# V through the other PSUM bank pair and VectorE, the front of each tile one iteration earlier, four tiles in the first three iterations

## The chip, the core and the metric

The kernel runs on one core of one Trainium2 chip. The metric is the device time of one execution in microseconds (us), the median of several runs. Engines are called as in the profile: PE is TensorE (PEld its weight load), DVE is VectorE, ACT is ScalarE, POOL is GpSimd, and SP is the queue that issues nearly all DMAs. PSUM has eight banks of 128 x 512 floats.

## What is computed

Two layers with residuals on x of 4 x 2048 x 256 floats, cut to what matters:

```
x0 = layernorm(x)                       # no weights
xn = layernorm(x0) * ln1_w + ln1_b
q, k, v = xn @ wq + bq, xn @ wk + bk, xn @ wv + bv     # 16 heads of 16
fq, fk = elu(q) + 1, elu(k) + 1
kv = einsum('bhnd,bhne->bnde', fk, v)   # for each token n over its heads
qkv = einsum('bhnd,bnde->bhne', fq, kv)
attn = qkv / (fq . (fk summed over the heads) + 1e-6)
y = x0 + attn @ wo + bo
h = gelu((layernorm(y) * ln2_w + ln2_b) @ fc_w + fc_b)
z1 = x + y + h @ proj_w + proj_b
z = layernorm(z1)
gates = softmax of the top 2 of 8 experts, from the mean of z over the 2048 tokens of a sequence
out = z1 + sum over experts of gate * gelu(z @ expert_w + expert_b)
```

(In the kernel the sum in the denominator comes out of the same matmuls as `qkv`, through a column of ones beside V.)

## The kernel before

The 8192 tokens are cut into 16 tiles of 512. A tile passes through stages, and each iteration of a hand-written schedule runs stages of several tiles. `LAG` says how many iterations behind its own number a tile reaches a stage: with LAG 0 iteration i works on tile i, with LAG 2 on tile i - 2. `iterations()` lists the stages of each iteration in order, and `walk()` replays that list for every engine, so each engine executes the stages that it has a part in, in exactly this order. An engine waits at semaphores; `INC` tells how much each stage adds to each of them, and `at(name)` is the value that a semaphore has when all stages ahead in the list are done. Nothing reorders: whoever waits holds all that stands behind it on the same engine. The stages that the change and the prediction speak of:

- **L** loads x of a tile (SP) into a ring of 4. **DS** takes its statistics (DVE, with the power on POOL), **D1** normalizes it (DVE) to `xhat`, **X** transposes it (PE) and ACT copies it to `xhT`. X, DV, DQ and DK are called the front of a tile here.
- **DV** multiplies V (PE) into the banks `sa` (two of the four banks of `ps`). ACT copies them to `feat_v` (L480), POOL adds the bias `bv` (L430), and SP stores the result to DRAM in eight DMAs (L327). `feat_v` is one buffer: ACT waits for the stores of the tile before (`v_out`). **DQ** and **DK** multiply Q and K (PE, into `pw` and `sa`), ACT and DVE make elu + 1 of them (`fqk`), SP stores them in two DMAs each (L333).
- **K0**, **K1** load the halves of q and k back in another layout (SP, 8 DMAs each, L356), behind the landing of all q and k stores listed ahead of them (`q_out`, `k_out`). **VL** loads V back (SP, 8 DMAs, L345).
- **B0**, **B8** are the scores of half 0 (PE, all four banks `ps`, masked by DVE at L658). **B1** to **B4** (merged with the MLP's rounds C1 to C4 as M1 to M4) are: B1 the weighted sums of half 0, B2 the scores of half 1, B3 the weighted sums of half 1. ACT evicts the sums to `ot`, **NS0**, **NS1** store them, **NL0**, **NL1** load them back transposed (SP).
- **N0** divides half 0 on DVE (L687, L690), **N** half 1, and casts and splits the result for a float32r matmul (L697, L698). **A2** multiplies it by w_o (PE, L986) into `sb`, the other two banks of `ps`, and DVE adds it to the residual (L708). **R** normalizes on DVE, **H** transposes (PE), M1 to M4, **J7** are the MLP.
- **Z** normalizes, **E** transposes z (PE, into `sb`) and ACT evicts it to `zT` (L518). **G** is the pooled gate at the end of a batch (iterations 7, 11, 15, the head iterations). **F1**, **F3**, **F2** are the experts.
- **WV** makes the bias `bv`, **WS** multiplies ln2_b by the MLP's weights (PE, L850) and folds and splits the weights on DVE (L631 to L643). It is in iteration 1, between the first and the second tile.

A full iteration (7 to 15) is `MERGED` and then a tail:

```python
TAIL = ["DV", "DQ", "DK", "A2", "F1", "R", "B0", "F3", "F4", "SA", "H", "B8", "FX", "F2"]
HEAD_TAIL = ["XL", "E", "X", "J7", "JA", "YB", "G", "N", *TAIL]
FULL_TAIL = ["XL", "X", "J7", "JA", "YB", "E", "N", *TAIL]
```

In iterations 3 to 6 (`EARLY`) A2 stands ahead of DK.

## Time and profile before

| | |
|---|---|
| median of 3 runs | 1098.13 us (1096.04 to 1101.01) |
| the profiled execution | 1095.77 us, its span 1093.9 us |
| PE busy | 953.9 us, 87% |
| DVE busy | 701.5 us, 64% |
| ACT busy | 472.2 us, 43% |
| POOL busy | 238.4 us, 22% |

Times in the trace are us from the start of the span. The first MLP round (M1) starts at 115.30 in iteration 3; a full iteration takes 56 to 60 us, a head iteration 64 to 67. A row of a timeline is start, duration, engine, line, operation, output<-inputs, and how many instructions were merged; in brackets stands how long the engine was idle before it and what it waited for. SPq is SP's DMA queue: its duration is that of issuing, not that of the transfer. The granted clock of PE is at one of two levels, 1.2 or 2.4 GHz.

### The profile page before, as it was taken

How to read it: one execution, taken by the hardware profiler on the slowest of the kernel's cores; microseconds unless marked ns; L12 is line 12 of the kernel's file. 1: busy time of each engine (PE TensorE's matmuls, PEld its weight loads, DVE VectorE, ACT ScalarE, POOL GpSimd, SP SyncE). 2: the span in 40 equal slices, each digit the busy share in tenths (PEclk: the TensorE clock that was granted, in tenths of full speed). 3: DMA queues.
4: the chain of work that ended last, by engine and by line, in shares of the span. 5: the costliest groups of instructions: out<-in, count | busy, mean ns of one | idle time of the engine just before them, and what ended most of it. 6: DMA issues, size and time to landing. Idle time of an engine off the chain costs nothing.

```text
span 1093.9 us, 29184 instructions
## 1 busy us (share of the span) xinstructions
PE 953.9 (87%) x12212; PEld 737.0 (67%) x12212; DVE 701.5 (64%) x1560; ACT 472.2 (43%) x738; POOL 238.4 (22%) x144
## 2 busy tenths in 40 slices
PE   4764888989698989999999989999999899897866
PEld 3543776768586767768686857777777768685633
DVE  2724565766557567777868586777777775856523
ACT  2321444535253444545545434545454454342422
POOL 3220132311314131312222131223131220312000
PEclk9866887989698889999999999999999899898979
DMA  5667354555545465565656574565666555431013
GB/s 178 106 131 120 85 91 100 98 117 95 119 89 91 105 121 122 104 159 88 150 108 130 125 131 113 112 148 107 143 107 137 110 112 116 93 88 58 33 64 116
DMA packets 428696, 120.85 MB, mean 110 GB/s; under 512 B 389904, under 2 KB 414608, under 8 KB 428304
## 3 DMA queue, kind: packets, MB, share of 16 engines
q1 hardware_dynamic: 426256, 116.83, 50.9%
q10 hardware_dynamic: 2304, 2.11, 0.7%
q8 instruction: 98, 1.61, 0.6%
q14 instruction: 38, 0.31, 0.1%
HBM read 60.17 MB, written 58.72 MB: 109 GB/s over the span
## 4 chain that ended last, share of the span: by engine, by line
PE 65%; DVE 18%; issue 8%; DMA 3%; ACT 3%; POOL 2%; SPq 1%; ACTq 0%; DVEq 0%; POOLq 0%
PE pw L936 18%; PE pj L920 13%; PE ps L892 7%; PE pw L840 5%; PE ps L986 4%; PE pj L840 4%; PE ps L905 4%; DVE nd L690 4%; DVE nd L687 4%; PE ps L872 3%; PE ps L881 2%; DVE hT L698 2%; DVE x_sb L723 2%; DVE hT L697 2%; PE pj L1030 1%
## 5 line engine op out<-in xcount | busy, mean ns | idle before, releaser
L936 PE MATMUL pw<-hT,w_fc 128*128 128x512 f32 x768 | 213.7, 419 | 10.4 <-DVE hT L678 10.4
L920 PE MATMUL pj<-w_pj,hidden 128*128 128x256 f32 x1536 | 208.7, 285 | 2.7 <-DVE hidden L671 2.7
L920 PEld LDWEIGHTS pj<-w_pj,hidden 128*128 128x128 f32 x1536 | 197.5, 190 | 14.1 <-DVE hidden L671 3.7
L671 DVE TENSOR_TENSOR hidden<-xhT,hidden 128x512 fp32r<-128x512 f32 x128 | 88.5, 692 | 165.2 <-ACT hidden L506 165.1
L505 ACT ACTIVATE xhT<-pw,col 128x512 f32<-128x512 f32 x128 | 87.8, 686 | 228.4 <-PE pw L936 227.0
L936 PEld LDWEIGHTS pw<-hT,w_fc 128*128 128x128 f32 x768 | 144.3, 199 | 43.0 <-DVE hT L678 12.1
L658 DVE TENSOR_TENSOR am<-ps,mask 128x512 f32<-128x512 f32 x128 | 79.3, 681 | 63.7 <-PE ps L892 63.7
L892 PE MATMUL ps<-kq 16*64 16x64 f32 x4096 | 87.8, 314 | 20.9 <-issue 10.9
L892 PEld LDWEIGHTS ps<-kq 16*64 16x64 f32 x4096 | 77.3, 210 | 42.4 <-issue 40.4
L986 PE MATMUL ps<-w_o,hT 128*128 128x256 f32 x384 | 61.5, 326 | 31.6 <-DVE hT L698 31.1
L506 ACT ACTIVATE hidden<-pw,col 128x512 fp32r<-128x512 f32 x128 | 87.1, 680 | 0.0
L986 PEld LDWEIGHTS ps<-w_o,hT 128*128 128x128 f32 x384 | 57.3, 229 | 43.7 <-DVE hT L698 28.5
L436 POOL TENSOR_TENSOR x<-x,row 128x1024 f32<-128x1024 f32 x16 | 37.7, 2354 | 216.3 <-DVE x_sb L723 216.3
L513 ACT ACTIVATE ot<-ps,den_eps 128x512 f32<-128x512 f32 x64 | 69.4, 1192 | 33.7 <-PE ps L905 32.7
L872 PE MATMUL ps<-w_qkv,xhT 128*128 128x256 f32 x256 | 70.2, 436 | 3.2 <-ACT xhT L470 3.2
L840 PE MATMUL pw<-zT,w_e 128*128 128x512 f32 x128 | 60.6, 618 | 8.1 <-DMA b_e<-in_eb 8.1
L430 POOL TENSOR_TENSOR feat_v<-feat_v,bv 128x512 f32<-128x512 f32 x32 | 52.7, 1664 | 56.1 <-ACT feat_v L480 56.1
L872 PEld LDWEIGHTS ps<-w_qkv,xhT 128*128 128x128 f32 x256 | 56.0, 225 | 13.0 <-issue 2.6
L840 PE MATMUL pj<-zT,w_e 128*128 128x512 f32 x128 | 58.7, 601 | 5.5 <-DVE out_sb L804 5.5
L651 DVE SCALAR_TENSOR_TENSOR fqk<-elu 128x512 f32<-128x512 f32 x64 | 44.4, 716 | 28.1 <-ACT elu L489 28.1
L687 DVE RECIPROCAL nd<-nd 128x256 f32<-128x256 f32 x32 | 55.8, 1744 | 8.9 <-DMA nd<-scratch_nd 8.9
L423 POOL TENSOR_TENSOR rs<-var,mhalf 128x8 f32<-128x8 f32 x16 | 28.2, 1764 | 151.8 <-DVE var L613 151.8
(108 smaller groups left out, 1307.8 us busy)
## 6 DMA issues: line engine op xcount, KB each, us to landing
scratch_nd<-ot SPq DMA_DIRECT2D x32, 512.0 KB, 4.4
nd<-scratch_nd SPq DMA_DIRECT2D x96, 128.0 KB, 2.6
x_sb<-in_x SPq DMA_DIRECT2D x16, 512.0 KB, 5.8
scratch_v<-feat_v SPq DMA_DIRECT2D x128, 64.0 KB
scratch_q<-fqk SPq DMA_DIRECT2D x32, 256.0 KB, 4.7
scratch_k<-fqk SPq DMA_DIRECT2D x32, 256.0 KB, 5.5
kq<-scratch_q SPq DMA_DIRECT2D x128, 64.0 KB, 3.1
kq<-scratch_k SPq DMA_DIRECT2D x128, 64.0 KB, 3.0
```

What stands on the lines that cost most here:

```text
L505: nc.scalar.activation(gelub[:, u], pw[u], ACT.Gelu, bias=b_fc[:, m:m + 1])
L506: nc.scalar.activation(hidden[:, m % SLOTS, 0], pw[u], ACT.Gelu, bias=b_fc[:, m:m + 1]).then_inc(S[f"pw_free{u}"], 1)
L513: nc.scalar.activation(dst[:, r // 2, v], src, ACT.Identity, bias=den_eps[:, :]).then_inc(S[f"sa_free{v}"], 1)
L658: last = nc.vector.tensor_tensor(am[:, j].rearrange("p (k n) -> p k n", n=BLOCK), ps[:, j].rearrange("p (k n) -> p k n", n=BLOCK), mask[:, ...
L671: nc.vector.tensor_tensor(hidden[:, m % SLOTS, 1], gelub[:, u], hidden[:, m % SLOTS, 0].bitcast(f32), ALU.subtract).then_inc(S["rest_ready ...
L687: link(nc.vector.reciprocal(d, d))
L840: last = nc.tensor.matmul(bank, w[:, c, P * m:P * (m + 1)], zT[:, p.t % RING, c], start=(c == 0), stop=(c == NC - 1))
L872: last = nc.tensor.matmul(sa[u][:, D * s:D * (s + 1)], xhT[:, c, P * (2 * u + s):P * (2 * u + s + 1)], w_qkv[:, 2, c], start=(c == 0), sto ...
L892: last = nc.tensor.matmul(ps[BLOCK * v:BLOCK * (v + 1), j, BLOCK * k:BLOCK * (k + 1)], kd[rows, b, cols], qd[rows, b, cols], start=True, s ...
L920: last = nc.tensor.matmul(pj[u][:, D * s:D * (s + 1)], hidden[:, m % SLOTS, a, lo:lo + P], w_pj[:, b, m], start=(m == 0 and n == 0 and s = ...
L936: last = nc.tensor.matmul(pw[bank], w_fc[:, b, c, P * m:P * (m + 1)], hT[:, a, c], start=(n == 0), stop=(n == len(order) - 1))
L986: last = nc.tensor.matmul(sb2[u][:, D * s:D * (s + 1)], attnT[:, a, c, lo:lo + P], w_o[:, b, c], start=(c == 0 and n == 0), stop=(c == NC ...
```

## The change

It has four parts. V is multiplied into the bank pair `sb` instead of `sa`, and one DVE instruction per bank takes it out and adds the bias; ACT's copy and POOL's addition are gone. The wait for the stores of the tile before moves with it, from ACT to DVE. The v stores on SP become a stage of their own, VS, and wait for DVE's instruction. The stages L to DK have LAG -1: iteration i does them for tile i + 1, so in the iterations from 3 on their place in the list is the same and their tile is the next one, and iteration 15 has none. The rings of x, of the q and k scratch and of the v scratch are one deeper. The lists of iterations 0 to 2 are new: they hold four fronts, K1 of tile 0 is now in iteration 1, and WS is in iteration 2.

```diff
-XRING = 4
+XRING = 5
+QKRING = 3
 X2RING = 1
-VRING = 2
+VRING = 3
...
-LAG = {"L": 0, "DS": 0, "D1": 0, "X": 0, "DV": 0, "DQ": 0, "DK": 0, "K0": 1, "K1": 1, "VL": 1, "B0": 1, "B8": 1,
+LAG = {"L": -1, "DS": -1, "D1": -1, "X": -1, "DV": -1, "VS": -1, "DQ": -1, "DK": -1, "K0": 1, "K1": 1, "VL": 1, "B0": 1, "B8": 1,
...
-TAIL = ["DV", "DQ", "DK", "A2", "F1", "R", "B0", "F3", "F4", "SA", "H", "B8", "FX", "F2"]
+TAIL = ["DV", "VS", "DQ", "DK", "A2", "F1", "R", "B0", "F3", "F4", "SA", "H", "B8", "FX", "F2"]
...
-    yield 0, ["WV", "DS:0", "L:1", "D1", "X", "DV", "DS:1", "DQ", "L:2", "D1:1", "DK"]
-    yield 1, ["X", "K0", "WS", "VL", "DV", "DQ", "DS:2", "DK", "D1:2", "B0", "B8", "K1"]
-    yield 2, ["K0", "Y", "B1", "NS0", "X", "DV", "B2", "NL0", "DQ", "B3", "NS1", "NL1", "VL", "N0", "K1",
-              "DK", "YB", "N", "A2", "R", "SA", "B0", "B8", "H"]
+    yield 0, ["WV", "DS:0", "L:1", "D1:0", "X:0", "DV:0", "VS:0", "DS:1", "DQ:0", "L:2", "D1:1", "DK:0"]
+    yield 1, ["X:1", "K0", "VL", "K1", "DV:1", "L:3", "DQ:1", "DS:2", "VS:1", "DK:1", "D1:2", "B0", "B8"]
+    yield 2, ["X:2", "DV:2", "Y", "B1", "NS0", "DQ:2", "B2", "NL0", "WS", "DS:3", "D1:3", "B3", "NS1", "N0", "DK:2", "K0", "NL1",
+              "VS:2", "X:3", "DV:3", "YB", "N", "VL", "VS:3", "DQ:3", "A2", "R", "K1", "DK:3", "SA", "B0", "B8", "H"]
...
-        yield i, MERGED + (HEAD_TAIL if i % PER_BATCH == PER_BATCH - 1 else FULL_TAIL)
+        names = MERGED + (HEAD_TAIL if i % PER_BATCH == PER_BATCH - 1 else FULL_TAIL)
+        yield i, [s for s in names if i < TILES - 1 or s not in ("L", "DS", "D1", "X", "DV", "VS", "DQ", "DK")]
...
-                if p.stage == "DV":
+                if p.stage == "VS":
                     wait("v_in", at("v_in", -INC["v_in"]["VL"]))
                     dst = v_dram[p.t % VRING].rearrange("(s b k g) d -> s b g k d", s=SUB, b=2, k=KG)
                     for s in range(SUB):
-                        wait("v_ready", at("v_ready", s // 2 + 1))
+                        wait(f"sb_free{s // 2}", at(f"sb_free{s // 2}"))
...
-                if p.stage == "DV":
-                    wait("pw_free0", INC["pw_free0"]["WV"])
-                    for u in range(2):
-                        wait(f"sa_free{u}", at(f"sa_free{u}", 1))
-                        half = feat_v[:, 2 * u:2 * u + 2]
-                        nc.gpsimd.tensor_tensor(half, half, bv[:, :].unsqueeze(1).broadcast_to([P, 2, D]),
-                                                ALU.add).then_inc(S["v_ready"], 1)
...
-                    wait("acc_ready", at("acc_ready"))
-                    wait("v_out", at("v_out"))
-                    for u in range(2):
-                        wait(f"sa_full{u}", at(f"sa_full{u}", 1))
-                        nc.scalar.activation(feat_v[:, 2 * u:2 * u + 2].rearrange("p s d -> p (s d)"), sa[u],
-                                             ACT.Identity).then_inc(S[f"sa_free{u}"], 1)
...
+                if p.stage == "DV":
+                    wait("acc_ready", at("acc_ready"))
+                    wait("v_out", at("v_out"))
+                    for u in range(2):
+                        wait(f"sb_full{u}", at(f"sb_full{u}", 1))
+                        nc.vector.tensor_tensor(feat_v[:, 2 * u:2 * u + 2], sb2[u].rearrange("p (s d) -> p s d", d=D),
+                                                bv[:, :].unsqueeze(1).broadcast_to([P, 2, D]),
+                                                ALU.add).then_inc(S[f"sb_free{u}"], 1)
...
                 if p.stage == "X":
                     wait("xhat_ready", at("xhat_ready"))
+                    wait("sc_free", at("sc_free"))
...
                     for u in range(2):
-                        wait(f"sa_free{u}", at(f"sa_free{u}"))
+                        wait(f"sb_free{u}", at(f"sb_free{u}"))
...
                     if "B" in parts and r == 1:
                         empty("sa")
+                        empty("sb")
                         wait("kq_in1", at("kq_in1"))
```

What stands in a row on SP in iteration 2 before, from NS0 of tile 0 on (then come V and K1; `nd` is the attention result, `scratch_v` the v stores, `scratch_q` and `scratch_k` the q and k stores, `kq` the loads of K0 and K1):

```order
L363 DMA scratch_nd<-ot 2048x1x64
L327 DMA scratch_v<-feat_v 8x8x256 x8
L369 DMA nd<-scratch_nd 128x4x64 x3
L333 DMA scratch_q<-fqk 128x16x32 x2
L363 DMA scratch_nd<-ot 2048x1x64
L369 DMA nd<-scratch_nd 128x4x64 x3
L345 DMA vb<-scratch_v 16x64x16 x8
```

And in the changed program, from the same NS0 on:

```order
L365 DMA scratch_nd<-ot 2048x1x64
L335 DMA scratch_q<-fqk 128x16x32 x2
L371 DMA nd<-scratch_nd 128x4x64 x3
L365 DMA scratch_nd<-ot 2048x1x64
L335 DMA scratch_k<-fqk 128x16x32 x2
L358 DMA kq<-scratch_q 16x2x512 x4
L358 DMA kq<-scratch_k 16x2x512 x4
L371 DMA nd<-scratch_nd 128x4x64 x3
L329 DMA scratch_v<-feat_v 8x8x256 x8
L347 DMA vb<-scratch_v 16x64x16 x8
```

The k stores of tile 2 and the eight K0 loads of tile 1 have moved ahead of the second load of `nd` (NL1), and the v stores of tile 2 from ahead of the first to behind the second.

What stands in a row on DVE at the end of iteration 2 before, with what each waits for, from the first division (N0) to the first instruction of A2's eviction:

```order
L687 RECIPROCAL nd<-nd 128x4x64 [waits num_in0]
L690 TENSOR_TENSOR nd<-nd 128x4x64 [waits dve_chain]
L690 TENSOR_TENSOR nd<-nd 128x4x64
L651 SCALAR_TENSOR_TENSOR fqk<-elu 128x512 [waits sa_free0,k_out,dve_chain]
L651 SCALAR_TENSOR_TENSOR fqk<-elu 128x512 [waits sa_free1]
L687 RECIPROCAL nd<-nd 128x4x64 [waits num_in1]
L690 TENSOR_TENSOR nd<-nd 128x4x64 [waits dve_chain]
L690 TENSOR_TENSOR nd<-nd 128x4x64
L697 CAST hT<-nd 128x1024 [waits dve_chain]
L698 TENSOR_TENSOR hT<-nd,hT 128x1024 [waits dve_chain]
L708 TENSOR_TENSOR x<-x,ps 128x512 [waits sb_full0,yb_ready]
```

And in the changed program, from the same first division on:

```order
L683 RECIPROCAL nd<-nd 128x4x64 [waits num_in0]
L686 TENSOR_TENSOR nd<-nd 128x4x64 [waits dve_chain]
L686 TENSOR_TENSOR nd<-nd 128x4x64
L647 SCALAR_TENSOR_TENSOR fqk<-elu 128x512 [waits sa_free0,k_out,dve_chain]
L647 SCALAR_TENSOR_TENSOR fqk<-elu 128x512 [waits sa_free1]
L620 TENSOR_TENSOR feat_v<-ps,bv 128x512 [waits sb_full0,v_out,acc_ready]
L620 TENSOR_TENSOR feat_v<-ps,bv 128x512 [waits sb_full1]
L683 RECIPROCAL nd<-nd 128x4x64 [waits num_in1]
L686 TENSOR_TENSOR nd<-nd 128x4x64 [waits dve_chain]
L686 TENSOR_TENSOR nd<-nd 128x4x64
L693 CAST hT<-nd 128x1024 [waits dve_chain]
L694 TENSOR_TENSOR hT<-nd,hT 128x1024 [waits dve_chain]
```

The two adds to V of tile 3 stand between the K features of tile 2 and the second division, and the first of them waits for `v_out`, the landing of all v stores that are listed ahead. WS and the statistics of tile 3 stand right ahead of the first row.

On PE in a full iteration, behind the transposes of z (the rows of L828), V before:

```order
L828 MATMUL ps<-ident,hn 128x128 [waits sb_free1]
L828 MATMUL ps<-ident,hn 128x128 x3
L872 MATMUL ps<-w_qkv,xhT 128x256 [waits sa_free0,sa_free1]
L872 MATMUL ps<-w_qkv,xhT 128x256 x3
L872 MATMUL ps<-w_qkv,xhT 128x256 [waits sa_free1]
```

And in the changed program:

```order
L828 MATMUL ps<-ident,hn 128x128 [waits sb_free1]
L828 MATMUL ps<-ident,hn 128x128 x3
L869 MATMUL ps<-w_qkv,xhT 128x256 [waits sb_free0,sa_free1,sa_free0]
L869 MATMUL ps<-w_qkv,xhT 128x256 x3
L869 MATMUL ps<-w_qkv,xhT 128x256 [waits sb_free1]
```

V now waits for the banks that the transposes ahead of it fill and ACT evicts, too.

## Rows read from the trace of the kernel before

**Rows 1.** Timeline of iteration 10 (start us, us, engine, line, operation, count, idle before).

```profile
568.94 3.62 PE L872 MATMUL ps<-w_qkv,xhT 128*128 128x256 f32 x16
569.19 0.20 ACT L518 ACTIVATION_READ_ACCUMULATOR zT<-ps 128x1 f32 x1
...
575.83 3.60 PE L881 MATMUL ps<-xhT,w_qkv 128*128 128x512 f32 x8
...
579.50 3.12 PE L986 MATMUL ps<-w_o,hT 128*128 128x256 f32 x24
579.67 5.05 SPq L327 DMA_DIRECT2D scratch_v<-feat_v  x8
...
587.02 1.26 ACT L545 ACTIVATE feat_v<-pw,b_e 128x512 f32<-128x512 f32 x2 [1.28 <-DMA scratch_v<-feat_v]
```

**Rows 2.** Timeline of iteration 3, from the cast to the next M1.

```profile
154.65 3.11 POOL L430 TENSOR_TENSOR feat_v<-feat_v,bv 128x512 f32<-128x512 f32 x2
155.00 1.64 DVE L697 CAST hT<-nd 128x1024 fp32r<-128x1024 f32 x1
...
156.67 2.17 DVE L698 TENSOR_TENSOR hT<-nd,hT 128x1024 fp32r<-128x1024 f32 x1
...
158.89 5.49 PE L986 MATMUL ps<-w_o,hT 128*128 128x256 f32 x24 [4.29 <-DVE hT L698]
...
175.94 5.46 PE L936 MATMUL pw<-hT,w_fc 128*128 128x512 f32 x12 [1.96 <-DVE hT L678]
```

**Rows 3.** Timeline of iteration 2, from NL1 to A2.

```profile
92.41 1.47 SPq L369 DMA_DIRECT2D nd<-scratch_nd  x3
...
96.03 1.75 DVE L687 RECIPROCAL nd<-nd 128x256 f32<-128x256 f32 x1 [5.19 <-DMA nd<-scratch_nd]
...
98.61 0.69 DVE L697 CAST hT<-nd 128x1024 fp32r<-128x1024 f32 x1
99.34 1.23 DVE L698 TENSOR_TENSOR hT<-nd,hT 128x1024 fp32r<-128x1024 f32 x1
...
100.71 5.46 PE L986 MATMUL ps<-w_o,hT 128*128 128x256 f32 x24 [12.97 <-DVE hT L698]
```

**Rows 4.** Timeline of SP's queue in iteration 1.

```profile
43.78 8.06 SPq L345 DMA_DIRECT2D vb<-scratch_v  x8
51.89 5.46 SPq L327 DMA_DIRECT2D scratch_v<-feat_v  x8
...
59.60 3.60 SPq L333 DMA_DIRECT2D scratch_k<-fqk  x2
66.69 1.72 SPq L356 DMA_DIRECT2D kq<-scratch_q  x4
```

**Rows 5.** Timeline of DVE, statistics of the first tile, and the weights.

```profile
7.67 0.42 DVE L588 BATCH_NORM_STATS2 stat<-x_sb 128x6 f32<-128x256 f32 x1
...
11.67 1.38 DVE L598 TENSOR_SCALAR xhat<-x_sb,mv,rs 128x256 f32<-128x256 f32 x4 [1.84 <-POOL rs L423]
...
35.66 0.16 DVE L631 TENSOR_TENSOR col<-col,pw 128x8 f32<-128x8 f32 x1 [3.66 <-PE pw L850]
...
38.25 1.22 DVE L641 CAST w_fc<-zT 128x2048 fp32r<-128x2048 f32 x1
39.50 2.29 DVE L643 TENSOR_TENSOR w_fc<-zT,w_fc 128x2048 fp32r<-128x2048 f32 x1
41.71 2.29 DVE L641 CAST w_pj<-zT 128x2048 fp32r<-128x2048 f32 x1
```

**Rows 6.** The page's part 5: busy, mean ns of one, idle before.

```profile
L658 DVE TENSOR_TENSOR am<-ps,mask 128x512 f32<-128x512 f32 x128 | 79.3, 681 | 63.7 <-PE ps L892 63.7
```

**Rows 7.** Timeline of PE in iteration 4, its A2.

```profile
219.75 4.53 PE L986 MATMUL ps<-w_o,hT 128*128 128x256 f32 x24 [3.51 <-DVE hT L698]
```

**Rows 8.** Timeline of iteration 15, the split and A2.

```profile
876.53 2.17 DVE L698 TENSOR_TENSOR hT<-nd,hT 128x1024 fp32r<-128x1024 f32 x1
...
882.07 3.42 PE L986 MATMUL ps<-w_o,hT 128*128 128x256 f32 x24
```

More of the change, by code:

```diff
@@ L51 @@
 EARLY = ["L", "M1", "Y", "NS0", "M2", "NL0", "K0", "DS", "M3", "NS1", "D1", "M4", "NL1", "VL", "N0", "K1", "X", "J7", "JA", "YB",
-         "N", "DV", "DQ", "A2", "R", "DK", "SA", "B0", "B8", "H"]
+         "N", "DV", "VS", "DQ", "A2", "R", "DK", "SA", "B0", "B8", "H"]
 def experts(t):
@@ L101 @@
 INC = {
-    "sa_full0": {"X": 1, "DV": 1, "DK": 1, **rounds("sa_full0")}, "sa_free0": {"X": 1, "DV": 1, "DK": 1, **rounds("sa_free0")},
-    "sa_full1": {"X": 1, "DV": 1, "DK": 1, **rounds("sa_full1")}, "sa_free1": {"X": 1, "DV": 1, "DK": 1, **rounds("sa_free1")},
-    "sb_full0": {"E": 1, "A2": 1}, "sb_free0": {"E": 1, "A2": 1}, "sb_full1": {"E": 1, "A2": 1}, "sb_free1": {"E": 1, "A2": 1},
+    "sa_full0": {"X": 1, "DK": 1, **rounds("sa_full0")}, "sa_free0": {"X": 1, "DK": 1, **rounds("sa_free0")},
+    "sa_full1": {"X": 1, "DK": 1, **rounds("sa_full1")}, "sa_free1": {"X": 1, "DK": 1, **rounds("sa_free1")},
+    "sb_full0": {"DV": 1, "E": 1, "A2": 1}, "sb_free0": {"DV": 1, "E": 1, "A2": 1}, "sb_full1": {"DV": 1, "E": 1, "A2": 1}, "sb_free1": {"DV": 1, "E": 1, "A2": 1},
     "pw_full0": {"WV": 1, "WS": 1, "DQ": 1, "F1": 1, "H": 1, "G": 1, **rounds("pw_full0")},
@@ L117 @@
     "f_ready": {"DQ": NC, "DK": NC},
-    "q_out": {"DQ": 32}, "k_out": {"DK": 32}, "v_out": {"DV": 16 * 2 * SUB},
+    "q_out": {"DQ": 32}, "k_out": {"DK": 32}, "v_out": {"VS": 16 * 2 * SUB},
     "kq_in0": {"K0": 32 * NQ}, "kq_in1": {"K1": 32 * NQ}, "v_in": {"VL": 32 * TA},
@@ L124 @@
     "z_ready": {"Z": 1},
-    "bv_ready": {"WV": 1}, "v_ready": {"DV": 2}, "pool_ready": {"G": 1}, "logit_ready": {"G": 1}, "gexp_ready": {"G": 1}, "gate_ready": {"G": 1},
+    "bv_ready": {"WV": 1},  "pool_ready": {"G": 1}, "logit_ready": {"G": 1}, "gexp_ready": {"G": 1}, "gate_ready": {"G": 1},
     "acc_ready": {"P": 1, "F1": 2, "F4": 2},
@@ L256, in build @@
         pj = [ctx.enter_context(nc.psum_tensor(f"pj{n}", [P, 512], f32)) for n in range(2)]
-        qk_dram = [nc.dram_tensor(f"scratch_{n}", (2, 4 * NQ, D, HALF // 2), f32, kind="Internal").ap() for n in "qk"]
+        qk_dram = [nc.dram_tensor(f"scratch_{n}", (QKRING, 4 * NQ, D, HALF // 2), f32, kind="Internal").ap() for n in "qk"]
         x2_dram = nc.dram_tensor("scratch_x2", (TILES, P, SUB, D), f32, kind="Internal").ap()
@@ L332, in run @@
                             wait("f_ready", at("f_ready", m + 1))
-                            sp.dma_start(qk_dram[n][p.t % 2].rearrange("u (c p) t -> c p u t", p=P)[m],
+                            sp.dma_start(qk_dram[n][p.t % QKRING].rearrange("u (c p) t -> c p u t", p=P)[m],
                                          fqk[:, NC * n + m].rearrange("p (u t) -> p u t", t=HALF // 2)
@@ L353, in run @@
                     for n, dst in ((0, qd), (1, kd)):
-                        src = qk_dram[n][p.t % 2].rearrange("(j b v) (d h) t -> j b d v (h t)", b=2, v=2, h=H)
+                        src = qk_dram[n][p.t % QKRING].rearrange("(j b v) (d h) t -> j b d v (h t)", b=2, v=2, h=H)
                         for j in range(NQ):
@@ L868, in run @@
                     for u in range(2):
-                        wait(f"sa_free{u}", at(f"sa_free{u}"))
+                        wait(f"sb_free{u}", at(f"sb_free{u}"))
                         for s in range(2):
                             for c in range(NC):
-                                last = nc.tensor.matmul(sa[u][:, D * s:D * (s + 1)], xhT[:, c, P * (2 * u + s):P * (2 * u + s + 1)], w_qkv[:, 2, c],
+                                last = nc.tensor.matmul(sb2[u][:, D * s:D * (s + 1)], xhT[:, c, P * (2 * u + s):P * (2 * u + s + 1)], w_qkv[:, 2, c],
                                                         start=(c == 0), stop=(c == NC - 1))
-                        last.then_inc(S[f"sa_full{u}"], 1)
+                        last.then_inc(S[f"sb_full{u}"], 1)
                 if p.stage in PARTS:
```

## The prediction

> **What bounds the kernel now.** I read the timeline of one full iteration first, then one of iterations 3 to 6, then the first 116 us. PE is busy for 87% of the span, so what matters is where it stands still, and the reader is to see three regimes. In the full iterations without the pooled head (8, 9, 10, 12, 13, 14) PE's queue is full: the K projection ends at 579.43 and the attention output projection, A2, starts at 579.50 [rows 1]. In iterations 3 to 6 PE stands for 4.29 and three times 3.51 us before A2 and waits for DVE, which divides and splits the attention result; A2 then takes 5.49 at a granted clock of 1.2 GHz, and 3.12 at 2.4 GHz [rows 1, 2, 7]. In iteration 2 it stands for 12.97 us [rows 3], and all around that a chain of SP's DMA issues and of DVE work sets the pace. The change touches all three, and its fourth tile goes into the third.
>
> **Part 1, what the fourth tile meets in the first iterations.** I follow the order of SP and DVE from a point that is the same in both programs: SP's loads of V for tile 0, 43.78 to 51.84 [rows 4]. Behind them now come the K1 loads of tile 0 (two groups like that at 66.69, 3.6 with their gaps), x of tile 3 (one issue, taken at 0.8), the q stores of tile 1 (2.2, from 57.35 to 59.60) and its eight v stores (5.46): all issued at 64.0. Eight v stores that were issued by 584.72 had landed at 587.02, 2.3 later [rows 1], so feat_v is free at 66.3.
> Only then can DVE take V of tile 2 out of PSUM. This is the new wait: all that is queued behind on DVE waits for the v stores of the tile before. The two adds take 0.7 each (512 columns with a PSUM operand took 681 ns [rows 6]): 67.7. The scores of tile 0's second half need those banks, 2.4: 70.1. The weight matmuls behind them cost 3.7, for DVE waited 3.66 for them: 73.8. Now DVE folds and splits the weights. At 35.66 this took 6.05 up to the cast of w_pj; that cast and its subtraction are as large as those of w_fc, 1.22 and 2.29, so 9.7 in all: 83.5 (beside GpSimd's add the cast took 2.29 [rows 5], which is gone). Behind it stand the statistics and xhat of tile 3 (5.4, as from 7.67 to 13.05 [rows 5]): 88.9, the first division N0 (2.6, like 96.03 to 98.61 [rows 3]): 91.5, and the two K features of tile 2 (1.3): 92.8.
> SP waits for these, because the k stores of tile 2 stand ahead of everything that iteration 2 still needs. The last issue takes 1.1: 93.9; landing 3.5 after the issue (63.20 to 66.69 [rows 4]): 97.4; the K0 loads of tile 1, which wait for it, 3.6: 101.0; the second load of the attention result, NL1, 1.5 [rows 3]: 102.5; the v stores of tile 2, 5.1 (as at 579.67 [rows 1]): 107.6; landing 2.3: 109.9. DVE's adds for V of tile 3 stand ahead of the second division: 111.2. Division, cast and split take 4.7 (96.03 to 100.71 [rows 3]): A2 starts at 115.9 and not at 100.71. The extra X, V and Q of tile 3 on PE, some 15 us at 1.2 GHz, fit below this chain and cost nothing; without the chain they would be what is late next. K of tile 3 stands behind A2, as in iteration 3, where M1 began 17.05 after A2 [rows 2]. So M1 of iteration 3 starts at 133.0 instead of 115.30, the first row behind the head: **+17.7**. Ends: +22, if the DMA issues of SP run one us per group slower; +3, if the v stores hold nobody, for then only K behind A2 is left.
>
> **Part 2, iterations 3 to 6.** GpSimd's add to V, 3.11, lies beside the cast and the subtraction that feed A2, 1.64 and 2.17 [rows 2]. With GpSimd idle the same two take 0.69 and 1.23 [rows 3]. The add is gone: 1.9 saved. The first of DVE's two new adds must be over before A2's first matmul: 0.7 paid. (The second lies beside A2's first half.) Net 1.2, four times, **-5.0** with the roundings.
> The Trainium skill has a rule for such rows (SBUF — State Buffer, the port arbitration): GpSimd and a VectorE instruction with two SBUF inputs take a shared port pair in turn, each for a whole instruction. By that rule the new adds, with an operand in PSUM, never wait for GpSimd, and the sum stays as it is; were the slow rows due to something that stays, it would be the last rival below.
> PE's gap before A2 shrinks in iterations 4 to 6 from 3.5 to 1.8 (V starts 0.5 later, part 3). At 2.4 GHz A2 would save 2.4, in iteration 4, where it took 4.53 [rows 7], 1.4: 6.2 if the clock stays up. Gaps of 1.5 with thin work behind them were followed by 1.2 GHz in three iterations of four; a gap under 1 us between dense work never was. I take two thirds, **-4.1**; ends 0 and -23.
>
> **Part 3, the full iterations.** V now goes to the banks that the transposes of z have just left. ScalarE is done with the first of them at 569.39, and PE began V at 568.94 [rows 1]: it must wait 0.45 to 0.5. DVE is in time for A2, with 1.9 less behind GpSimd and 1.3 more for the adds. PE has no slack, so 0.44 goes through six times: **+2.6**; ends 0 (a later wait takes it up) and +4. In the head iterations 7 and 11 the transposes of z come first and PE holds A2: nothing. ScalarE loses two copies of 0.6 per tile; it waits for PE before and behind them: nothing. SP's v stores start behind its K loads as before: nothing.
>
> **Part 4, iteration 15** loses its front. X lay beside DVE's work. V, Q and K filled the time between the gate matmuls and A2 at 882.07; now A2 waits for the subtraction, which began at 876.53 [rows 8] and takes 1.23: 877.8, 4.3 earlier. PE then has stood for over 8 us, so A2 takes 2.4 more and the expert matmuls 0.2: **-1.7**; ends 0 and -5. The front is worth some 12 us of PE, but DVE's chain takes its place.
>
> **The sum** is 17.7 - 5.0 - 4.1 + 2.6 - 1.7 = +9.5. The profiled execution took 1095.77 (span 1093.9 and 1.9 around it), which gives 1105.3. It lies 2.4 under the median of the three runs, 1098.13; the result is a median, so the forecast is put on that: **1107.6 us**.
>
> **Rivals.** *Idle time is filled*, as the order looks at first sight: SP is ahead of my count and the v stores hold nobody. For it: PE stands from 87.7 to 100.7, longer than a front needs. Against: the store stands ahead of the adds, and the adds ahead of the division. Sum 3 - 5.0 - 4.1 + 2.6 - 1.7 = -5.2: 1092.9. It decides from where A2 of iteration 2 starts before 101.
> *The clock stays up*: in iterations 3 to 6 A2 (2.4), the scores (1.0) and the first up projection (5.4 against 3.0) run at 2.4 GHz, 5.8 four times, 23 in place of 4.1. Against: the gap before M1 isn't touched. Sum -9.6: 1088.5. This is the one on the other side of no change; it decides from where 14 of the 23 come.
> *The clock falls as before*, for a gap of 1.8 is enough: no 4.1: 1111.7.
> *SP falls further behind*: part 1 is 22 and the clock anywhere between: 1112 to 1116.
> *GpSimd is not what slows the cast*: then A2 comes 0.7 later, not 1.2 earlier, in iterations 3 to 6 (+7.8), the clock falls (+4.1), and the full iterations pay 0.65 instead of 0.44 (+1.3): 1120.8.
>
> **How the numbers follow.** Forecast 0.45 (own range 1101 to 1113), idle time filled 0.15, clock up 0.12, clock falls 0.13, SP behind 0.11, not GpSimd 0.04. 1093 to 1116 leaves out the clock case, the lower half of the filled one and the last, 2 in 10. About 0.5%, 5.5 us, is what a measurement tells from no change. Faster than 1092.6: the clock case and part of the filled one, 0.18. Slower than 1103.6: most of the forecast and the last three, 0.64. Between: 0.18.
>
> **What would show it.** Right: A2 of iteration 2 starts near 116, DVE stands before its adds for tile 3 until the v stores land, SP issues NL1 after 100, M1 of iteration 3 starts near 133; cast and subtraction take 0.7 and 1.2; PE's gap before A2 in iterations 4 to 6 is under 2; V starts half a microsecond behind the transposes of z; A2 of iteration 15 waits for DVE. Wrong: A2 of iteration 2 before 105 (part 1), one clock throughout iterations 3 to 6 (part 2), V right behind the transposes (part 3), A2 of iteration 15 as long behind the gate matmuls as before (part 4).

## The result: 1118.3 us, and the profile after

The changed kernel takes 1118.32 us (median of 4 runs, 1115.11 to 1122.02), the kernel before beside it on the same chip 1097.09 (4 runs, 1095.77 to 1101.01). The ratio is 1.0196, 95% interval 1.0158 to 1.0235: some 21 us slower, where +9.5 was forecast. The profiled execution took 1115.74 with a span of 1113.9; that of before had 1093.9. So it is these 20.0 us that have to be found in the traces.

Rows from parts 1 and 2 of the page of the changed kernel: busy time and share of each engine, then PE's busy share and its granted clock in 40 slices, each in tenths.

```profile
PE 948.9 (85%) x12212; PEld 732.5 (66%) x12212; DVE 701.3 (63%) x1592; ACT 454.5 (41%) x706; POOL 185.9 (17%) x112
PE   5655578897989789999999989999999869897966
PEclk9865689799989899999999999999999979898989
```

The work has moved as it should: ACT and POOL have less. But PE's share is 85%, where it was 87, and PE is thinnest and its clock lowest in slices 3 to 5, 56 to 139 us, the end of iteration 1 and iteration 2. I set M1, the first MLP matmul of each iteration, against its place before, as start after minus start before:

```
M1 of iteration          3      7      8      15     16
before, us            115.30 357.18 423.57 833.81 897.56
after, us             153.13 381.20 445.61 857.58 919.13
after - before         +37.8  +24.0  +22.0  +23.8  +21.6
```

Behind M1 of iteration 16 another 1.6 comes back: 37.8 - 13.8 - 2.0 + 1.8 - 2.2 - 1.6 = 20.0. The first iterations cost 37.8 us and not 17.7, and iterations 3 to 6 return 13.8 and not 9.1. The full iterations and iteration 15 come near the forecast in their sums, +1.8 and -2.2 for +2.6 and -1.7, the first of them by luck (below). Iteration 7 and the end, which the forecast put at nothing, give back 2.0 and 1.6.

**The first iterations**, step by step. DVE's timeline of the changed kernel (start us, us, engine, line, operation, out<-in, count, idle before and what ended it):

```profile
59.09 0.42 DVE L576 BATCH_NORM_STATS2 stat<-x_sb 128x6 f32<-128x256 f32 x1 [16.53 <-issue]
...
73.99 0.69 DVE L620 TENSOR_TENSOR feat_v<-ps,bv 128x512 f32<-128x512 f32 x1 [6.84 <-PE ps L869]
...
83.24 2.48 DVE L654 TENSOR_TENSOR am<-ps,mask 128x512 f32<-128x512 f32 x4 [0.37 <-PE ps L889]
89.09 0.17 DVE L627 TENSOR_TENSOR col<-col,pw 128x8 f32<-128x8 f32 x1 [3.37 <-PE pw L846]
...
98.62 0.42 DVE L576 BATCH_NORM_STATS2 stat<-x_sb 128x6 f32<-128x256 f32 x1
...
102.53 5.41 DVE L586 TENSOR_SCALAR xhat<-x_sb,mv,rs 128x256 f32<-128x256 f32 x4 [1.75 <-POOL rs L425]
107.86 1.74 DVE L683 RECIPROCAL nd<-nd 128x256 f32<-128x256 f32 x1
...
110.43 1.29 DVE L647 SCALAR_TENSOR_TENSOR fqk<-elu 128x512 f32<-128x512 f32 x2
128.08 1.29 DVE L620 TENSOR_TENSOR feat_v<-ps,bv 128x512 f32<-128x512 f32 x2 [16.35 <-DMA scratch_v<-feat_v]
```

PE's timeline of the same kernel:

```profile
67.25 1.94 PE L824 MATMUL ps<-ident,xhat 128*128 128x128 f32 x8 [19.36 <-issue]
...
77.14 3.70 PE L878 MATMUL pw<-xhT,w_qkv 128*128 128x512 f32 x8
80.77 2.42 PE L889 MATMUL ps<-kq 16*64 16x64 f32 x128
83.13 5.86 PE L846 MATMUL pw<-col,zT 128*128 128x1 f32 x32
...
133.91 5.36 PE L984 MATMUL ps<-w_o,hT 128*128 128x256 f32 x24 [13.81 <-DVE hT L694]
...
153.13 3.22 PE L933 MATMUL pw<-hT,w_fc 128*128 128x512 f32 x7 [2.00 <-DVE hT L674]
```

SP's DMA issues of the same kernel:

```profile
41.46 8.69 SPq L347 DMA_DIRECT2D vb<-scratch_v  x8
...
54.54 0.43 SPq L314 DMA_DIRECT2D x_sb<-in_x  x1
...
111.15 1.34 SPq L335 DMA_DIRECT2D scratch_k<-fqk  x2
116.25 1.72 SPq L358 DMA_DIRECT2D kq<-scratch_q  x4
...
119.89 1.52 SPq L371 DMA_DIRECT2D nd<-scratch_nd  x3
121.46 4.95 SPq L329 DMA_DIRECT2D scratch_v<-feat_v  x8
```

The second half of the chain in the prediction is there, link by link: k stores of tile 2 (111.15), landing, K0 (116.25), NL1 (119.89), v stores (121.46), landing, adds (128.08), division, A2 (133.91). The forecast had the end of the K features to A2 as 92.8 to 115.9, 23.1 us; it took 22.2, from 111.72 to 133.91. Of the 20.1 us that part 1 missed, 18.9 lie ahead of it, between 52 and 112 us; another 2.1 come behind A2, where PE stops for 2.23 us within its scores (148.69). DVE idles 16.53 us until 59.09, before the statistics of tile 2, and PE 19.36 us until 67.25, before the transposes of tile 2. What ends both is "issue", nothing that the profile shows. But SP loads x of tile 3 at 54.54, and the statistics begin 4.5 us behind that issue. That load is for another tile; what ties them together is in the code (below).

**Iterations 3 to 6.** DVE and PE of the changed kernel in iteration 4, from the cast to A2:

```profile
251.42 0.69 DVE L693 CAST hT<-nd 128x1024 fp32r<-128x1024 f32 x1
...
252.15 1.23 DVE L694 TENSOR_TENSOR hT<-nd,hT 128x1024 fp32r<-128x1024 f32 x1
...
253.29 1.28 DVE L620 TENSOR_TENSOR feat_v<-ps,bv 128x512 f32<-128x512 f32 x2
254.12 3.07 PE L984 MATMUL ps<-w_o,hT 128*128 128x256 f32 x24 [1.63 <-DVE feat_v L620]
```

Cast and subtraction take 0.69 and 1.23, as forecast, PE's gap before A2 is 1.63 where [rows 2, 7] have 4.29 and 3.51, and A2 takes 3.07. The stretches from A2 of iterations 4, 5 and 6 to the next A2, before and then after (us from:to, length, PE busy, matmuls, mean granted clock, DMA share, GB/s):

```profile
219.75:278.89 59.14, 50.82 (x737) 0.93 0.54 108
278.89:340.48 61.59, 53.18 (x737) 0.86 0.52 97
340.48:407.79 67.31, 59.97 (x748) 0.83 0.53 110
```

```profile
254.12:309.99 55.87, 49.46 (x737) 0.97 0.59 111
309.99:366.88 56.89, 51.35 (x736) 0.91 0.55 106
366.88:429.85 62.97, 54.99 (x749) 0.92 0.59 121
```

From A2 of iteration 3 to that of iteration 7 the changed kernel needs 13.5 us less. The gaps before A2 are 5.6 shorter (three of 3.51 that are now 1.63); the other 7.9 come with a granted clock of 0.91 to 0.97 in place of 0.83 to 0.93. Cut at M1 and A2, the 13.8 of iterations 3 to 6 are 5.7 from M1 to A2 and 8.1 from A2 to the next M1. Of the 8.1, A2 itself gives 6.3: in iterations 4, 5 and 6 it takes 3.07, 3.07 and 3.10 where it took 4.53, 5.49 and 5.48. The other 1.8 come in iteration 5, where PE in the kernel before stopped for 1.43 us within its scores (at 292.97) and in the changed kernel doesn't. The fall to 1.2 GHz doesn't vanish, it becomes rarer.

**The full iterations and iteration 15.** PE in iteration 10, then around A2 of iteration 15:

```profile
595.13 3.69 PE L869 MATMUL ps<-w_qkv,xhT 128*128 128x256 f32 x16 [0.43 <-ACT zT L506]
...
605.13 3.38 PE L984 MATMUL ps<-w_o,hT 128*128 128x256 f32 x24
...
892.22 1.02 PE L998 MATMUL pw<-w_g,hn 128*128 128x8 f32 x4 [4.70 <-DVE hn L737]
901.58 5.49 PE L984 MATMUL ps<-w_o,hT 128*128 128x256 f32 x24 [8.34 <-DVE hT L694]
```

V waits 0.43 us for ACT's `zT`, against none in [rows 1]; A2 of iteration 15 waits 8.34 for the subtraction. Both are what the prediction wrote.

The sum of +1.8 hides larger terms. From A2 of iteration 7 to that of iteration 8 the changed kernel needs 60.57 us at a granted clock of 0.97, the kernel before 56.99 at 1.00. PE stops within the scores of iteration 8:

```profile
455.66 1.03 PE L889 MATMUL ps<-kq 16*64 16x64 f32 x38 [1.87 <-issue]
456.62 2.93 PE L917 MATMUL pj<-w_pj,hidden 128*128 128x256 f32 x12
```

The projection behind the stop takes 2.93 us; in the next round the same twelve matmuls take 1.58. All seven kernels of this document whose fronts run one iteration ahead have this stop, 1.3 to 2.3 us long, and need 59.6 to 63.5 us for the stretch; the five others don't have it and need 56.4 to 57.4. So it belongs to the new lists. The profile shows nothing that ends it, and its cause stays open.

### The profile page after: what moved, and what is told of

It is laid out like the page before. It is cut to its first block, busy times and chain, and to the rows that moved or that the text cites. A ratio compares the mean times of both kernels' runs of the same rounds, so it can differ in the third digit from the quotient of the medians.

```text
span 1113.9 us, 29151 instructions
## 1 busy us (share of the span) xinstructions
PE 948.9 (85%) x12212; PEld 732.5 (66%) x12212; DVE 701.3 (63%) x1592; ACT 454.5 (41%) x706; POOL 185.9 (17%) x112
## 4 chain that ended last, share of the span: by engine, by line
PE 73%; DVE 12%; issue 7%; DMA 2%; ACT 2%; POOL 2%; SPq 1%; ACTq 0%; DVEq 0%; POOLq 0%
PE pw L933 18%; PE pj L917 15%; PE ps L889 7%; PE pw L836 4%; PE ps L869 4%; PE ps L878 4%; PE ps L984 4%; PE pj L836 4%; PE ps L902 4%; PE pw L878 3%; DVE nd L683 2%; DVE nd L686 2%; PE pj L1028 1%; DVE am L654 1%; PE pw L824 1%
## 5 line engine op out<-in xcount | busy, mean ns | idle before, releaser
L984 PE MATMUL ps<-w_o,hT 128*128 128x256 f32 x384 | 59.0, 316 | 33.4 <-DVE hT L694 25.4
L984 PEld LDWEIGHTS ps<-w_o,hT 128*128 128x128 f32 x384 | 54.0, 215 | 43.0 <-DVE hT L694 24.6
L878 PE MATMUL ps<-xhT,w_qkv 128*128 128x512 f32 x128 | 60.9, 620 | 1.3 <-ACT ot L501 1.3
L686 DVE TENSOR_TENSOR nd<-nd 128x256 f32<-128x256 f32 x64 | 58.4, 953 | 1.1
L878 PE MATMUL pw<-xhT,w_qkv 128*128 128x512 f32 x128 | 57.6, 593 | 0.0
```

Of the source, the lines that this page charges most:

```text
L686: last = nc.vector.tensor_tensor(n, n, d, ALU.mult)
L878: last = nc.tensor.matmul(bank, w_qkv[:, j // NC, c, P * (j % NC):P * (j % NC + 1)], xhT[:, c], start=(c == 0), stop=(c == NC - 1))
L984: last = nc.tensor.matmul(sb2[u][:, D * s:D * (s + 1)], attnT[:, a, c, lo:lo + P], w_o[:, b, c], start=(c == 0 and n == 0), stop=(c == NC ...
```

## Experiments

The kernel before was measured on the same chip beside each group of kernels; its medians were 1096.35 us (first four experiments), 1096.85 (next four) and 1099.63 (last two), so I give the ratio with its 95% interval beside each time.

### The change cut in two: V's path alone, the lists alone

Of the diff, `values_alone` keeps V's banks, the evicting engine, `VS` and the rings. The fronts and the first iterations are those of before:

```diff
-LAG = {"L": -1, "DS": -1, "D1": -1, "X": -1, "DV": -1, "VS": -1, "DQ": -1, "DK": -1,
+LAG = {"L": 0, "DS": 0, "D1": 0, "X": 0, "DV": 0, "VS": 0, "DQ": 0, "DK": 0,
...
-    yield 1, ["X:1", "K0", "VL", "K1", "DV:1", "L:3", "DQ:1", "DS:2", "VS:1", "DK:1", "D1:2", "B0", "B8"]
+    yield 1, ["X", "K0", "WS", "VL", "DV", "VS", "DQ", "DS:2", "DK", "D1:2", "B0", "B8", "K1"]
```

> The lists of stages, the fronts and the number of tiles in the first iterations are those of the kernel before; V alone goes to the other bank pair and is taken out by VectorE with its bias. Theory A (the changed path of V brings what the changed kernel gained in iterations 3 to 6, and the first iterations' lists cost what it lost): M1 of iteration 3 stays near 115.3, some 14 to 16 us are gained up to the M1 behind iteration 7, 1.8 is lost again in the full iterations: 1081 to 1086. Theory of the prediction, taken literally (its parts 2 and 3 without 1 and 4): 1097 - 9.1 + 2.6 = 1090.6. Rival (the gain belongs to the front that is one iteration further ahead): no gain here, 1097 to 1100.

Measured: 1080.47 us (6 runs, 1075.51 to 1083.24), ratio 0.9857 (0.9825 to 0.9888). M1 of iteration 3 comes 1.5 earlier than before, that of iteration 8 15.4 earlier, the end 15.8. The time is 0.5 us below the forecast range. Theory A holds; this half of the change makes the kernel faster by 16 us.

`lists_alone` has the lists, fronts and rings of the changed kernel, with V through ACT and POOL in `sa`:

```diff
-                        wait(f"sb_free{u}", at(f"sb_free{u}"))
+                        wait(f"sa_free{u}", at(f"sa_free{u}"))
...
+                        nc.scalar.activation(feat_v[:, 2 * u:2 * u + 2].rearrange("p s d -> p (s d)"), sa[u],
+                                             ACT.Identity).then_inc(S[f"sa_free{u}"], 1)
...
+                        nc.gpsimd.tensor_tensor(half, half, bv[:, :].unsqueeze(1).broadcast_to([P, 2, D]),
+                                                ALU.add).then_inc(S["v_ready"], 1)
```

> The reverse: lists, fronts and rings of the changed kernel, but V through ScalarE and GpSimd in the old bank pair. Theory A: the first iterations cost 35 to 38 as in the changed kernel and nothing comes back in iterations 3 to 6; iteration 15 gives 2: 1128 to 1134. Rival (gain of iterations 3 to 6 belongs to the front further ahead): 1116 to 1121, like the changed kernel.

Measured: 1126.06 us (4 runs, 1122.62 to 1128.03), ratio 1.0281 (1.0243 to 1.0319), 2 us below the forecast. M1 of iteration 3 comes 33.3 later than before; iterations 3 to 6 return 3.2, not 13.8. So what they gain in the changed kernel belongs to V's path, and the loss in the first iterations to the lists. The halves do not quite add up: at M1 of iteration 3 it is +33.3 and -1.5 apart, +37.8 together. In `lists_alone` PE waits 7.67 us before A2 and in the changed kernel 13.81: there it is ACT that stands before `feat_v` until the v stores land, and DVE divides meanwhile, from 125.89 on and not from 129.28. With V's path changed DVE stands there itself, the wait that the prediction named. And xhat of tile 3 takes 1.38 us there, with no POOL add beside it, where the changed kernel has 5.41.

### x of tile 3, one place later

DVE's statistics wait for `at("x_in")`, which is the count of *all* loads listed ahead of them. The new list names L:3 ahead of DS:2, so the statistics of tile 2 wait for x of tile 3, which SP issues behind 24 DMAs for tile 0 (K0, VL, K1). The experiment moves only this:

```diff
-    yield 1, ["X:1", "K0", "VL", "K1", "DV:1", "L:3", "DQ:1", "DS:2", "VS:1", "DK:1", "D1:2", "B0", "B8"]
+    yield 1, ["X:1", "K0", "VL", "K1", "DV:1", "DQ:1", "DS:2", "L:3", "VS:1", "DK:1", "D1:2", "B0", "B8"]
```

> The changed kernel with one stage moved: the load of x of tile 3 stands behind the statistics of tile 2 in iteration 1 and not ahead of them. Theory B (the statistics of tile 2 count all loads listed ahead of them and so wait for x of tile 3, which SP issues only behind the loads of tile 0): they start at 43 and not at 59.1, X of tile 2 long before 67, V of tile 2 is taken out at 67 when the v stores have landed and not at 74, and with the Q projection out of the way the scores end near 70.5 and not at 83.2: A2 of iteration 2 near 121 and not at 133.9, the whole near 1105.5. Rival (another chain, SP's, is as long): VectorE starts earlier but A2 moves by less than 6, the whole above 1112.

Measured: 1106.30 us (4 runs, 1102.52 to 1109.52), ratio 1.0105 (1.0068 to 1.0142). DVE's timeline of this kernel, and A2 on PE:

```profile
43.10 0.42 DVE L576 BATCH_NORM_STATS2 stat<-x_sb 128x6 f32<-128x256 f32 x1
...
67.04 1.29 DVE L620 TENSOR_TENSOR feat_v<-ps,bv 128x512 f32<-128x512 f32 x2 [15.88 <-DMA scratch_v<-feat_v]
```

```profile
68.69 2.43 PE L889 MATMUL ps<-kq 16*64 16x64 f32 x128 [4.12 <-DVE feat_v L620]
...
123.08 5.46 PE L984 MATMUL ps<-w_o,hT 128*128 128x256 f32 x24 [13.33 <-DVE hT L694]
```

The statistics start right behind the K features, 16.0 us earlier; V of tile 2 now waits for the v stores, until 67.04. The prediction had 66.3 for that: its chain up to here was right for a kernel without the wait that it overlooked. A2 comes 10.8 earlier. Theory B holds, with A2 2 us behind the place that was expected.

### The v stores of tile 2 and NL1 ahead of the K stores

```diff
-    yield 2, [..., "NL0", "WS", "DS:3", "D1:3", "B3", "NS1", "N0", "DK:2", "K0", "NL1",
-              "VS:2", "X:3", "DV:3", "YB", "N", ...]
+    yield 2, [..., "NL0", "VS:2", "WS", "DS:3", "D1:3", "B3", "NS1", "NL1", "N0", "DK:2", "K0",
+              "X:3", "DV:3", "YB", "N", ...]
```

> The changed kernel with two stages moved on SP in iteration 2: the v stores of tile 2 go out as soon as V of tile 2 is there (ahead of the weights), and NL1, the second load of the attention result, ahead of the K stores and K0. Theory C (from 110 to 134 the chain is k stores, landing, K0, NL1, v stores, landing, adds, division): the adds of V of tile 3 come at 116 to 118 when PE has V, the division right behind them, A2 of iteration 2 at 122.5 and not at 133.9: the whole near 1107. Rival (PE, with X, V and Q of tile 3, is as late): A2 after 129, the whole above 1114.

Measured: 1102.93 us (8 runs, 1100.21 to 1108.63), ratio 1.0070 (1.0037 to 1.0103). SP, DVE and PE of this kernel:

```profile
88.02 5.32 SPq L329 DMA_DIRECT2D scratch_v<-feat_v  x8
...
97.59 1.47 SPq L371 DMA_DIRECT2D nd<-scratch_nd  x3
```

```profile
117.66 0.69 DVE L620 TENSOR_TENSOR feat_v<-ps,bv 128x512 f32<-128x512 f32 x1 [1.80 <-PE ps L869]
...
122.89 4.61 PE L984 MATMUL ps<-w_o,hT 128*128 128x256 f32 x24 [1.84 <-issue]
```

The stores go out 33 us earlier and DVE's adds wait for PE alone. A2 comes at 122.89 (122.5 expected). The time is 4 below what was expected; in the traces the end comes 12.2 earlier, little more than A2. Theory C holds.

### Both, and then the weights where they were

> The changed kernel with both mends: x of tile 3 loaded behind the statistics of tile 2, and the v stores of tile 2 and NL1 ahead of the K stores. If the two chains are in series they add: A2 of iteration 2 at 133.9 - 10.8 - 11.0 = 112.1, the whole at 1118.3 - 12.0 - 15.4 = 1091. Rival (behind both there is one more chain, PE's X, V and Q of tile 3 at 1.2 GHz behind the weights): A2 not before 117, the whole above 1095.

Measured: 1094.90 us (10 runs, 1087.38 to 1096.87), ratio 0.9977 (0.9947 to 1.0006); A2 of iteration 2 at 110.97. The two waits are in series and their costs add: three moved names in the lists were worth 23 us. The time is 4 above what was expected and the place of A2 1 below.

The next kernel also lists `WS` in iteration 1 behind K0, as before:

> As the two mends together, and the weights are folded and split in iteration 1 again, where they stood before the change. Theory (they take 7.0 on PE and 9.5 on VectorE between the scores and xhat of tile 3): A2 of iteration 2 at 100 to 103, M1 of iteration 3 at 118 to 120, so the fourth tile costs only what stands behind A2, +3 to +5, and iteration 15 gives 2 back: 1080 to 1085, no better than the kernel with V's path alone (1080.5). Rival (the idle time is worth a whole front): 1074 or less.

Measured: 1083.74 us (6 runs, 1080.25 to 1085.02), ratio 0.9885 (0.9847 to 0.9923). A2 of iteration 2 on PE:

```profile
95.39 3.08 PE L984 MATMUL ps<-w_o,hT 128*128 128x256 f32 x24 [1.83 <-issue]
```

It starts 5.3 earlier than before and 5 to 8 earlier than the 100 to 103 that were expected, and M1 of iteration 3 2.2 earlier: up to here the fourth tile costs nothing. The time is in the expected range, but by way of an earlier start and a later loss. The kernel is no faster than V's path alone, which takes the front of tile 3 an iteration later. At M1 of iteration 8 it is 1.8 ahead of that kernel (17.2 earlier than before, against 15.4). The stretches from A2 of iteration 7 to 8 and of 13 to 14 are then 3.2 and 4.9 longer than before. They ran at 0.97 and 0.92, and in both PE stops within the scores, for 1.58 us in the first and here in the second:

```profile
772.66 0.55 PE L889 MATMUL ps<-kq 16*64 16x64 f32 x13 [1.86 <-issue]
773.14 2.93 PE L917 MATMUL pj<-w_pj,hidden 128*128 128x256 f32 x12
```

V's path alone has one such stretch, 0.94, with a stop of 1.26. Iteration 15, which has no front now, gives back no more than 2, for DVE's chain takes the front's place.

### What is V's path worth, and what of it is only GpSimd's add?

The trace of the changed kernel has one more row that is slow beside POOL: the two products of the second division (L686) took 3.60 us in iterations 4 and 10, 0.76 in the first division. POOL's second add of YB lies beside them. It isn't needed before the sum of the MLP's end, so it can wait until DVE has split the result:

```diff
                     slot = x_sb[:, p.t % XRING]
+                    wait("attnT_ready", at("attnT_ready", 1))
                     nc.gpsimd.tensor_tensor(slot, slot, rows_of(D), ALU.add).then_inc(S["pool_chain"], 1)
```

> V's path alone, and GpSimd's second add of YB waits until the attention result is split. Theory D (in iterations 3 to 6 the two products of the division take 3.60 beside that add and 0.76 without it, and PE stands 1.6 before A2 for them): the products take 0.8 to 1.6, the gap before A2 goes to nothing in iterations 4 to 6, 2 us are gained in each of four iterations, and up to 3 more if the granted clock stays at 2.4 GHz longer: 1069 to 1074. Rival (the first add alone is enough to slow the products, or PE is waiting for the bank that A2 writes): no more than 2 gained, 1078 to 1081.

Measured: 1069.91 us (6 runs, 1066.88 to 1075.94), ratio 0.9763 (0.9721 to 0.9806). Iteration 4 of V's path alone, then of this kernel:

```profile
207.44 3.59 DVE L686 TENSOR_TENSOR nd<-nd 128x256 f32<-128x256 f32 x2
...
213.76 3.06 PE L984 MATMUL ps<-w_o,hT 128*128 128x256 f32 x24 [1.62 <-DVE feat_v L620]
```

```profile
204.15 1.45 DVE L687 TENSOR_TENSOR nd<-nd 128x256 f32<-128x256 f32 x2
...
207.67 2.38 POOL L435 TENSOR_TENSOR x_sb<-x_sb,row 128x1024 f32<-128x1024 f32 x1 [2.69 <-DVE hT L695]
208.34 3.35 PE L985 MATMUL ps<-w_o,hT 128*128 128x256 f32 x24
```

The products take 1.45 (the first add still touches them), and PE has no gap before A2. Theory D holds: one wait, 10.6 us in the medians and 8.6 in the traces, of which 7.2 are there by M1 of iteration 8. The clock gave nothing to it: the stretches from A2 of iterations 4, 5 and 6 ran at 0.91, 0.91 and 0.87, with V's path alone at 0.94, 0.91 and 0.84. No kernel of this document is faster; the next one is as fast within the noise.

> All three mends of the first iterations and the held second add together. If the fourth tile in the first iterations is worth its front, this is the fastest: 1066 to 1072; if it only moves work, it is within 3 us of the kernel with V's path alone and the held add.

Measured: 1071.65 us (6 runs, 1067.71 to 1076.50), ratio 0.9773 (0.9734 to 0.9811): within 3 us of the one without the fourth tile, which was the forecast for the case that the tile only moves work. The trace says how: at M1 of iteration 8 this kernel is 3.0 ahead of the other (25.6 earlier than before, against 22.6), and it loses that where all kernels with the new lists have their stops, from A2 of iteration 7 to 8 and of 13 to 14 (63.54 and 62.54 us, both at 0.92).

Then the reverse question: does V need other banks and another engine, or only a POOL that is silent at the right time? The kernel before, with one wait:

```diff
                     wait("pw_free0", INC["pw_free0"]["WV"])
+                    wait("attnT_ready", at("attnT_ready"))
                     for u in range(2):
```

> The kernel before, V through ScalarE and GpSimd as it was, and one wait added: GpSimd's add to V waits until VectorE has split the attention result. Theory E (what V's new path gains in iterations 3 to 6 is only that GpSimd no longer works beside the cast and the subtraction): the gap before A2 falls from 3.51 to 1.6 and all that follows from it comes too, while the full iterations don't pay the 0.4 for the other banks: 1080 to 1084. Rival (GpSimd's add, two to three us later, holds up the v stores and what SP has behind them, or collides with the next VectorE work): above 1088.

Measured: 1086.10 us (6 runs, 1079.93 to 1089.66), ratio 0.9881 (0.9833 to 0.9930). The cast, A2 and POOL's add in iteration 4:

```profile
212.50 0.69 DVE L698 CAST hT<-nd 128x1024 fp32r<-128x1024 f32 x1
...
214.51 3.08 PE L987 MATMUL ps<-w_o,hT 128*128 128x256 f32 x24 [1.63 <-DVE hT L699]
...
214.59 3.32 POOL L431 TENSOR_TENSOR feat_v<-feat_v,bv 128x512 f32<-128x512 f32 x2 [2.40 <-issue]
```

The gap is 1.63, as with V's path changed, and M1 of iteration 8 comes 13.9 earlier (15.4 there). At the end of the traces it is 10.6, against 15.8 there; the ratios, 0.9881 and 0.9857, overlap in their intervals. The time is 2 us above the forecast, with a before that is 3 above that of the other groups; 13.5 us are gained by one wait. Theory E holds: nearly all that V's path brings in iterations 3 to 6 is that POOL no longer works beside the cast and the subtraction.

> The same, and the second add of YB held as well. If both waits act as in the kernel with V's path alone and one held add (1069.9): 1068 to 1073. Rival (two adds of GpSimd, some 5.6 us, now stand together behind the split and beside the sums and statistics of x): above 1076.

Measured: 1080.23 us (6 runs, 1074.06 to 1087.46), ratio 0.9839 (0.9788 to 0.9890). That is 7 above the forecast and in the range of the rival. M1 of iteration 8 comes 24.8 earlier than before, more than in any other kernel but one, but M1 of iteration 12 only 16.6: the stretches from A2 of iterations 9 and 10 to the next ran at 0.94 and 0.90, and in both PE stops within the scores (1.25 us at 523.46, 2.18 at 584.79, both "issue"). With V's own path and the second add held, the lead falls only from 22.6 to 20.2. Whether the stops follow from POOL's adds, as the rival would have it, one trace of each kernel doesn't tell; it stays open.

## Why the prediction was wrong, and where it was right

**Part 1, the term that failed:** 17.7 forecast, 37.8 measured. The step that failed is the wait that was to let DVE take V of tile 2 out at 66.3: the prediction named the landing of the v stores, and the one that ended last was for V itself, held up by the statistics of tile 2, which waited for the load of x of tile 3. The steps, as the prediction put them, against the trace:

```
step                                     forecast  trace  late by
v stores of tile 1 issued                  64.0     64.6     0.6
V of tile 2 taken out                      67.7     76.5     8.8
scores of tile 0, half 1                   70.1     83.2    13.1
weight matmuls                             73.8     88.9    15.1
weights folded and split                   83.5     98.6    15.1
xhat of tile 3                             88.9    107.9    19.0
K features of tile 2                       92.8    111.7    18.9
A2 of iteration 2                         115.9    133.9    18.0
M1 of iteration 3                         133.0    153.1    20.1
```

*"This is the new wait: all that is queued behind on DVE waits for the v stores of the tile before."* The wait was there, but behind another that I had not looked for. I asked of V of tile 2 when its buffer is free, not when PE can have made it. The statistics of tile 2 counted the load of tile 3, and so PE had V at 74 and not at 66. `x3_later` shows that this wait alone costs 10.8 us at A2 (in the ratio 1.0105 against 1.0196): without it the v stores do hold DVE, until 67.0.

*"The scores of tile 0's second half need those banks, 2.4."* The Q projection of tile 2 stands between the two on PE, 3.70 us; I followed DVE and SP link by link and PE only where DVE waits for it. In `x3_later` that projection is over by 64.6, and the scores end at 71.1: its share goes with the wait. *"The weight matmuls behind them cost 3.7"* came from a wait of DVE, which sees only what of them is left; they took 5.86. (The 9.7 behind them adds up to 9.6 from its rows; it took 9.5.)

*"Behind it stand the statistics and xhat of tile 3 (5.4, as from 7.67 to 13.05 [rows 5])".* There xhat is alone; here both adds of YB lie beside it, and its four instructions take 5.41 in place of 1.38, behind a further 1.75 for the power on POOL. This is the same mechanism that part 2 rests on, in a place where I had taken a row from an undisturbed stretch. By the Trainium skill (SBUF — State Buffer, "Who interferes with whom") casts and `tensor_scalar` can run in a mode that takes both ports, and then they contend as an instruction with two SBUF inputs does. The trace agrees: the subtraction, the cast, the products and xhat were all slow beside a POOL add, while DVE's adds with a PSUM operand kept their 0.64 to 0.69 us.

`x3_later` shows how much each is worth when the overlooked wait is gone. Against the forecast its scores end 1.0 late, the weight matmuls 4.3 (78.1), xhat 8.1 (97.0) and A2 7.2. So of the 18.0 at A2 the overlooked wait made 10.8, and most of the rest are the weight matmuls and xhat.

From the K features to A2 the chain was right to 1 us, and M1 then came 19.2 behind A2, where 17.05 were forecast. `v2_nl1_early` shows that it could be cut, by 11.0 us at A2. The rival *SP falls further behind* put part 1 at 22 and had the wrong engine: the v stores of tile 1 were 0.6 late.

**Part 2:** -5.0 and -4.1 forecast, -13.8 measured. The mechanism was right, and `old_v_held` shows it apart. The first size was nearly right: M1 to A2 became 5.7 shorter for the forecast 5.0, and PE's gap came out at 1.63 for 1.8. The second was off: I took two thirds of the 6.2 that A2 alone could gain by the clock, and the whole of it came, 6.3. Another 1.8 came in iteration 5 and nowhere else; a stop of 1.43 us in the kernel before makes most of it, which no part of the prediction had. The up projection, which the rival *the clock stays up* had priced too, still ran at 1.2 GHz at M1 of iteration 6 (5.46 us for twelve matmuls).

**Part 3:** +2.6 forecast, +1.8 measured over iterations 8 to 14; that they are near is luck. The stretches from A2 of iterations 9, 12 and 13, which ran at 1.00 in both kernels, took 56.37, 56.39 and 57.43 us before and take 57.51, 57.68 and 58.82 now: 1.1 to 1.4 more, and not 0.44. The sum comes out low because the kernel before needed 60.16 at 0.97 from A2 of iteration 11 to 12, and the changed one 57.00 at 1.00. The term itself is there: V stands 0.43 behind ACT, A2 follows with 0.3 less, and against `lists_alone`, which has the same lists, the three stretches are 0.37 to 0.45 longer. The other 0.8 to 0.9 stand in `lists_alone` as well; but V's path alone is 0.7 to 1.0 longer than before there, so the two don't simply add, and the cause of what lies above 0.44 stays open.

**Part 4:** -1.7 forecast, -2.2 measured. A2 of iteration 15 was to come 4.3 earlier, and from M1 of iteration 15 to it the difference to before falls from +23.8 to +19.5, by 4.3; then 2.1 are paid back up to the next M1, where 2.6 were expected.

The answer "slower" was right. Part 1 missed by 20.1 us, and the total by only 10.5, since iterations 3 to 6 gave back 4.7 more than forecast, iteration 7 and the end 3.6 that I had put at nothing, and parts 3 and 4 together 1.3: errors that happened to lie the other way. One count of a semaphore is worth 12 of the 21 us (`x3_later`), and the two stages on SP that stood too late 15 (`v2_nl1_early`).

## What to carry to other kernels

A stage that waits for a running count waits for everything listed ahead of it: moving a load one place forward in such a list makes consumers of other tiles wait for it. When work is added to a stretch, walk all queues through it, also the one that looks idle, and take each duration from a row with the same neighbours. And before an engine is relieved for good, see whether its work can simply wait: one added wait on POOL brought 13.5 us, and another 10.6.
